# Sixteen experts on tiles of 64 slots instead of 128, two tiles side by side on TensorE's columns, in six streams that keep an expert's weights

## The chip, the cores and the metric

The kernel runs on one core of one Trainium2 chip. The metric is the device time of one execution in microseconds (us). A core has five engines that work at the same time and meet at semaphores: PE (TensorE, matrix products), DVE (VectorE), ACT (ScalarE), POOL (GpSimd) and SP, which mostly starts DMAs. PEld in the profile is the loading of PE's stationary operand. All numbers are float32 unless a row says otherwise. A float32 matmul shows up in the trace as two records, each with its own weight load; a transpose on PE shows up as one.

## The reference, cut to what matters

The program is one block of a graph network on 1250 nodes of 512 numbers: a performer block and a four-layer graph network, whose results are added to `x`, and then a mixture of experts. Only the last part is touched by the change:

```python
h = xf @ shared_w1 + shared_b1                      # shared expert, 384 hidden units
z = swiglu5(h, *shared_act) @ shared_w2 + shared_b2
gate_probs = softmax(xf @ gate_w + gate_b)          # 16 experts
w, idx = top_k(gate_probs, 2); w = w / sum(w)
he = einsum('nd,edh->enh', xf, expert_w1) + expert_b1     # w1: 512 x 768 per expert
te = swiglu5(he, expert_act)                        # gate and up are the even and odd columns
oe = einsum('enh,ehd->end', te, expert_w2) + expert_b2    # w2: 384 x 512 per expert
y = einsum('ne,end->nd', cw, oe)                    # cw: the two weights of a node, else 0
return y + z
```

Two experts per node are wanted, so 2500 rows (node, expert) have to be computed. With the inputs of the reference the gate is far from even. Rows by expert, 0 to 15: 71, 5, 1044, 7, 450, 335, 0, 2, 12, 2, 1, 13, 245, 0, 313, 0. That makes 29 tiles of 128 rows or 49 tiles of 64 rows, each tile of one expert.

## The kernel before, in words

The order of the work on each engine is written out by hand: each engine has its own list of instructions, and semaphores join them. Nothing is reordered by a scheduler.

`moe` has four parts. (1) Routing: `gate_pe`, `choose_dve`, `rank_pe` and `slots_dve` find each node's two experts, count the rows of each expert, round each count up to tiles, and give each row a slot. `slot_expert` holds, for each of the `SLOT_TILES` tiles, the number of its expert. POOL scatters the 2500 rows into `slot_dram` with 20 indirect DMAs (L1998). (2) Meanwhile PE computes the shared expert (`shared_pe`, L2179, and `shared_down_pe`, L2231 and L2233). (3) The expert loop, one tile per round. (4) The combination: the two results of each node are read back and added with their weights (L2438).

There are always 35 rounds in part 3, the most that any routing could need, and tiles beyond the last real one are computed too, with the last expert's weights. In round `i` of `experts_pe`, PE does: the first 512 columns of the up product of tile `i+1` (`up_pe`, L2306), the three transposes of tile `i`'s gated values (L2326), the other 256 up columns of tile `i+1` (L2306), the four transposes that turn the rows of tile `i+2` into columns (L2293), and the down product of tile `i` (L2337). `glu_dve` (L2350 to L2359) adds the bias, clips, and multiplies; `experts_act` makes the sigmoid (L2375) and the three copies out of PSUM (L2366, L2388, L2394); POOL scatters the tile's result (L2407). SP loads for every tile the expert's `w1` and `w2`, its bias row copied to 128 partitions, and its five constants (`load_up`), into rings of `U = 3` buffers, and the tile's rows (`load_slots`) into a ring of 10. It loads the weights again even where two tiles in a row are of the same expert.

The performer, a quite different part of the program, has one product (`attend`, L942) that puts two 64-column outputs on PSUM partitions 0 to 63 and 64 to 127, with different stationary and different moving operands, in turn.

Of the kernel before, what the change touches and what calls it, by code (L numbers as in the profile page):

```python
# [18 lines left out]
N = 1250  # L19
# [33 lines left out]
SLOT_TILES = (2 * N + EXPERTS * 127) // 128  # L53
# [58 lines left out]
def build(nc, a, out):  # L112
    with ExitStack() as ctx:
# [5 lines left out]
        slot_dram = nc.dram_tensor("slot_rows", [SLOT_TILES * 128, ROW], F32)  # L119
        outer = lambda name, shape: ctx.enter_context(nc.sbuf_tensor(name, shape, F32))  # L120
        w = [outer(f"w{i}", [128, KC, D]) for i in range(3)]
# [11 lines left out]
        with c.stage():  # L133
            moe(c, x, w, cols, rows, slot_dram, out)


def performer(c, xbuf, gnn_x, xn_dram, sum_dram, ln_count, cond_parts, cond_w_parts, w, cols, rows,
# [66 lines left out]
    with ExitStack() as ctx:  # L204
# [45 lines left out]
        blank = kf[0:112].rearrange("p a f -> p (a f)")[:, 0:ROW]  # L250
# [83 lines left out]
        def sp_start():  # L334
# [24 lines left out]
            for r0 in (0, 64):  # L359
# [4 lines left out]
            load(sp, slot_dram[:, :].rearrange("(p s) d -> p s d", p=112),  # L364
                 blank.unsqueeze(1).broadcast_to([112, SLOT_TILES * 128 // 112, ROW])).then_inc(c.slots_blank, 16)
# [949 lines left out]
def gnn(c, x, ln_count, cond_parts, cond_w_parts, w, y_cols, rows, sum_dram):  # L1315
# [28 lines left out]
    with ExitStack() as ctx:  # L1344
# [87 lines left out]
        def norm_dve(m, t):  # L1432
# [11 lines left out]
            if t >= 1:  # L1444
# [4 lines left out]
                if m == 2 * L - 1:  # L1449
                    v.wait_ge(norm_step, done + 1)  # L1450
                    v.tensor_scalar(v_rows[:, s, :], x[:, s, :], mv[:, s, 0:1], rstd[:, s:s + 1], ALU.subtract,
                                    ALU.mult).then_inc(normed, 1)
                    return
# [19 lines left out]
        def layer_sp(l):  # L1473
# [20 lines left out]
            if last:  # L1494
# [3 lines left out]
                for n, done in enumerate(((o_mm, NT * L), (h_mm, 12 * L))):  # L1498
                    sp.wait_ge(*done)
                    load(sp, w[n][:].rearrange("p c o -> p (c o)")[:, 0:4 * FFN_I].rearrange("p (c o) -> p c o", c=2),  # L1500
                         a["L0_ffn_shared_w1"].rearrange("(c p) o -> p c o", p=128)[:, 2 * n:2 * n + 2, :]).then_inc(
# [352 lines left out]
def moe(c, x, w, cols, rows, slot_dram, out):  # L1854
# [4 lines left out]
    U, S, R = SLOT_RING, SLOT_TILES, NT  # L1859
    TE = NT * EXPERTS  # L1860
    RANK, TOTAL, LOGIT, TURN, OUT = 6, 7, 5, 6, 7
    param_dram = nc.dram_tensor("swiglu_params", [EXPERTS + 1, 8], F32)
    back_dram = nc.dram_tensor("slot_outputs", [2 * N + S * 128, D], F32)
# [13 lines left out]
    up_in = [c.sem(f"e_up_in{u}") for u in range(U)]  # L1877
    down_in = [c.sem(f"e_down_in{u}") for u in range(U)]
# [7 lines left out]
    with ExitStack() as ctx:  # L1886
        sb = lambda name, shape, dt=F32: ctx.enter_context(nc.sbuf_tensor(name, shape, dt))
        ring = lambda name, shape: [sb(f"{name}{i}", shape) for i in range(U)]
        hidden = sb("m_hidden", [128, IC, N])
        ew1 = ring("m_ew1_", [128, KC, 2 * FFN_I])  # L1890
        ew2 = ring("m_ew2_", [128, IC, D])
# [20 lines left out]
        slot_id = sb("m_slot_id", [1, S])  # L1912
# [3 lines left out]
        ones = sb("m_ones", [P, P])  # L1916
        start_of = sb("m_start_of", [P, NT + 1, EXPERTS])
        place = sb("m_place", [P, NT, EXPERTS])
        total = sb("m_total", [P, EXPERTS])
        tiles_of = sb("m_tiles_of", [P, 3, EXPERTS])  # L1920
        pos_f = sb("m_pos_f", [P, 2, NT])
        pos = sb("m_pos", [P, 2 * NT], U32)
        passed = sb("m_passed", [1, S, EXPERTS])
        expert_f = sb("m_expert_f", [1, S])
        slot_expert = sb("m_slot_expert", [1, S], I32)
        slot_place = sb("m_slot_place", [128, S], I32)
        place_of = sb("m_place_of", [P, 2, NT])
        blank_place = sb("m_blank_place", [128, S])
# [577 lines left out]
```

## Time and profile before

| | us |
|---|---|
| Median of 3 runs (2779.07 to 2780.36) | 2779.67 |
| The profiled execution's own time | 2776.7 |
| Its span | 2775.0 |
| PE busy in it | 2667.2 |
| DVE busy | 1432.7 |
| ACT busy | 858.1 |
| POOL busy | 294.7 |

Busy times are sums over the span of one execution; PE's is that of pipelined matmuls whose ends are modelled, so a PE busy all the time is not shown to be at its peak. The rows further down are read with the line numbers of the kernel before. "us" after a start time is how long the merged instructions took, "xN" how many there are, and square brackets hold the engine's idle time ahead of the row and what ended it.

### The profile page before, as it was taken

How to read it: one execution, taken by the hardware profiler on the slowest of the kernel's cores; microseconds unless marked ns; L12 is line 12 of the kernel's file. 1: busy time of each engine (PE TensorE's matmuls, PEld its weight loads, DVE VectorE, ACT ScalarE, POOL GpSimd, SP SyncE). 2: the span in 40 equal slices, each digit the busy share in tenths (PEclk: the TensorE clock that was granted, in tenths of full speed). 3: DMA queues.
4: the chain of work that ended last, by engine and by line, in shares of the span. 5: the costliest groups of instructions: out<-in, count | busy, mean ns of one | idle time of the engine just before them, and what ended most of it. 6: DMA issues, size and time to landing. Idle time of an engine off the chain costs nothing. (4 is left out here: it accounts for less than half of the span.)

```text
span 2775.0 us, 28828 instructions
## 1 busy us (share of the span) xinstructions
PE 2667.2 (96%) x10335; PEld 1613.8 (58%) x10336; DVE 1432.7 (52%) x3252; ACT 858.1 (31%) x1813; POOL 294.7 (11%) x308
## 2 busy tenths in 40 slices
PE   7999889989999999999999999999999999999995
PEld 4554544435777555677655577655577754455552
DVE  8995651322666551566652466553366544433333
ACT  5654533210444211244211144312044322212221
POOL 3000012000200100100020200020010013311111
PEclk9999999999999999999999999999999999999997
DMA  5400101230000010000011100011000011669996
GB/s 165 147 21 11 38 8 45 69 106 31 23 1 1 21 37 31 23 1 1 0 39 35 37 2 1 1 39 34 32 7 1 1 46 31 235 232 391 389 378 226
DMA packets 105293, 203.78 MB, mean 73 GB/s; under 512 B 22273, under 2 KB 22803, under 8 KB 105151
## 3 DMA queue, kind: packets, MB, share of 16 engines
q1 hardware_dynamic: 94858, 182.11, 18.8%
q0 software_dynamic: 7600, 14.93, 1.5%
q10 hardware_dynamic: 2693, 4.89, 0.6%
q8 instruction: 84, 1.38, 0.2%
q14 instruction: 58, 0.48, 0.1%
HBM read 168.18 MB, written 31.66 MB: 72 GB/s over the span
## 5 line engine op out<-in xcount | busy, mean ns | idle before, releaser
L1784 ACT ACTIVATE g_prob<-g_prob,g_row_max 125x1250 f32<-125x1250 f32 x160 | 214.0, 1337 | 710.6 <-DVE g_row_max L1718 710.6
L1524 PE MATMUL psum<-cols,w 128*128 128x500 f32 (+1 forms) x1152 | 408.2, 514 | 6.8 <-PEq L81 6.8
L1586 PE MATMUL psum<-g_k_cols,g_q_cols 128*125 128x512 f32 (+1 forms) x960 | 362.9, 513 | 1.9 <-DVE g_row_max L1715 1.9
L1600 PE MATMUL psum<-cols,rows 125*128 125x250 f32 x1600 | 364.0, 374 | 0.1
L1524 PEld LDWEIGHTS psum<-cols,w 128*128 128x128 f32 x1152 | 216.5, 189 | 186.6 <-issue 178.5
L1600 PEld LDWEIGHTS psum<-cols,rows 125*128 125x128 f32 x1600 | 302.6, 189 | 34.7 <-issue 3.8
L1715 DVE CUSTOM_DVE_ANT_0 g_prob<-psum,ln_count 125x1250 f32<-125x1250 f32 x160 | 233.4, 1459 | 75.0 <-PE psum L1586 75.0
L1586 PEld LDWEIGHTS psum<-g_k_cols,g_q_cols 128*125 128x125 f32 x960 | 168.0, 187 | 161.8 <-issue 159.1
L1725 DVE COPY cols<-psum 125x500 f32<-125x500 f32 x160 | 108.6, 678 | 198.8 <-PE psum L1615 198.8
L1615 PEld LDWEIGHTS psum<-ident,g_prob 125*125 125x125 f32 x1600 | 199.4, 188 | 9.0 <-issue 1.9
L1615 PE MATMUL psum<-ident,g_prob 125*125 125x125 f32 x1600 | 200.3, 272 | 0.0
L2306 PE MATMUL psum<-m_ew,m_x_cols 128*128 128x256 f32 (+1 forms) x560 | 191.9, 486 | 0.3 <-ACT m_x_cols L2366 0.3
L1838 POOL TENSOR_TENSOR xbuf<-xbuf,g_bias_rows 125x512 f32<-125x512 f32 x40 | 67.4, 1721 | 937.4 <-DVE rows L1460 937.4
L1690 DVE TENSOR_SCALAR g_k_cols<-psum,g_bias_cols 128x500 f32<-128x500 f32 (+1 forms) x48 | 31.3, 653 | 237.4 <-PE psum L1524 237.4
L1708 DVE TENSOR_SCALAR g_prob<-g_prob,g_row_max 125x1250 f32<-125x1250 f32 x160 | 145.5, 909 | 5.6
L2306 PEld LDWEIGHTS psum<-m_ew,m_x_cols 128*128 128x128 f32 x560 | 103.7, 190 | 72.5 <-issue 66.5
L1626 PE MATMUL psum<-w,g_q_cols 128*125 128x512 f32 x320 | 143.9, 592 | 0.0
L1672 PE MATMUL psum<-w,g_k_cols 128*125 128x512 f32 x320 | 143.6, 592 | 0.0
L1800 ACT COPY cols<-psum 125x500 f32<-125x500 f32 x320 | 134.3, 469 | 17.6 <-PE psum L1615 16.9
L1573 PE MATMUL psum<-w,cols 128*125 128x512 f32 x320 | 139.3, 592 | 0.0
L2350 DVE TENSOR_TENSOR m_work<-psum,m_eb 128x768 f32<-128x768 f32 x35 | 33.5, 958 | 173.4 <-PE psum L2306 173.4
L1834 POOL TENSOR_TENSOR xbuf<-xbuf,g_bias_rows 125x512 f32<-125x512 f32 x40 | 55.2, 1417 | 616.2 <-DMA g_bias_rows<-in_L_gnn_bo 616.2
(317 smaller groups left out, 3282.9 us busy)
## 6 DMA issues: line engine op xcount, KB each, us to landing
m_ew<-in_L_ffn_expert_w SPq DMA_DIRECT2D x35, 1536.0 KB
m_ew<-in_L_ffn_expert_w SPq DMA_DIRECT2D x35, 768.0 KB, 7.9
m_eb<-in_L_ffn_expert_b SPq DMA_DIRECT2D x35, 384.0 KB
slot_rows<-p_kf SPq DMA_DIRECT2D x1, 9240.0 KB, 34.1
rows<-slot_rows SPq DMA_DIRECT2D x35, 264.0 KB, 8.1
w<-in_L_gnn_m_w SPq DMA_DIRECT2D x8, 1024.0 KB
w<-in_L_mix_W SPq DMA_DIRECT2D x4, 1024.0 KB, 5.1
w<-in_L_gnn_wq SPq DMA_DIRECT2D x4, 1024.0 KB, 5.2
```

What stands on the lines that cost most here:

```text
L1524: ins = c.pe.matmul(c.bank(group_bank(g), width), wt[:, k, o * 128:(o + 1) * 128], y_cols[:, k, start:start + width], start=(k == 0), stop ...
L1573: ins = pe.matmul(c.bank(V_BANKS[t], D, P), y_cols[:, k, t * P:(t + 1) * P], w[2][:, k, :], start=(k == 0), stop=(k == KC - 1))
L1586: ins = pe.matmul(psum[0:P, start:start + width], q_cols[:, h, t * P:(t + 1) * P], k_cols[:, h, start:start + width], start=True, stop=True)
L1600: ins = pe.matmul(c.bank(6 + g % 2, 2 * P), v_rows[:, j, h * 128:(h + 1) * 128], turned_prob[:, g % 2, j, :], start=(j == 0), stop=(j == N ...
L1615: ins = pe.transpose(psum[0:P, b * BANK + j * P:b * BANK + (j + 1) * P], prob[:, u, (j0 + j) * P:(j0 + j + 1) * P], ident[0:P, 0:P])
L1626: ins = pe.matmul(c.bank(t % 2, D, P), q_cols[:, k, t * P:(t + 1) * P], w[0][:, k, :], start=(k == 0), stop=(k == KC - 1))
L1672: ins = pe.matmul(c.bank(t % 2, D, P), k_cols[:, k, t * P:(t + 1) * P], w[2][:, k, :], start=(k == 0), stop=(k == KC - 1))
L1708: v.tensor_scalar(prob[:, u, :], prob[:, u, :], row_max[:, u, 3:4], None, ALU.mult).then_inc(prob_made, 1)
L1715: v.tensor_tensor_reduce(prob[:, u, :], psum[0:P, 0:N], ln_count[:, t, :], 1.0, NOT_AN_EDGE / 10, ALU.add, ALU.max, row_max[:, u, 0:1]).th ...
L1784: s.activation(prob[:, u, :], prob[:, u, :], ACT.Exp, bias=row_max[:, u, 1:2], accum_out=row_max[:, u, 2:3]).then_inc(exp_made, 1)
L1800: s.copy(turned_prob[:, g % 2, j0:j0 + nj, half:half + P], by_chunk(c.bank(b, nj * P, P))).then_inc(turned_act, 1)
L2306: ins = pe.matmul(psum[0:128, at:at + cn], x_cols[u][:, k, :], ew1[u][:, k, c0:c0 + cn], start=(k == 0), stop=(k == KC - 1))
```

## The change

Tiles have 64 slots (`HALF`) in place of 128. There are `STREAMS = 6` streams of `TURNS = 9` tiles, 54 tiles in all, of which 49 are real. The tiles lie in order of expert, and stream `s` has tiles `9s` to `9s+8`. A round of the expert loop now treats a pair: the same turn of two neighbouring streams, on columns 0 to 63 and 64 to 127 of PE. There are 27 pairs; pair `i` is of streams 0 and 1, 2 and 3, or 4 and 5 by `i` modulo 3.

By the counts above the streams hold these experts:

```
stream 0: 0 0 1 2 2 2 2 2 2        stream 3: 4 4 5 5 5 5 5 5 7
stream 1: 2 2 2 2 2 2 2 2 2        stream 4: 8 9 10 11 12 12 12 12 14
stream 2: 2 2 3 4 4 4 4 4 4        stream 5: 14 14 14 14 15 15 15 15 15
```

Each stream has one buffer for `w1` and `w2` of its expert. The first six are loaded by SP (`load_first_weights`); the buffers of streams 3 to 5 lie in memory that the shared expert uses before, so SP loads stream 3 after the shared up product and streams 4 and 5 after the shared down product. From then on POOL issues for every tile but a stream's last one indirect gather for `w1` after the pair's up product and one for `w2` after its down product. Where the next tile has the same expert, 127 of the 128 row numbers are made too large and are skipped, so that one row of 12 KB or 6 KB is still moved. For this the rows of `w1` and `w2` go to partitions in runs ("(p c)" in place of "(c p)"), and the layer norm ahead permutes its output columns to match. The biases are now loaded in two halves of 64 partitions, the rows in two halves too. The bias add writes gate and up values apart, so the clips after it read runs.

```diff
+HALF = 64
+STREAMS = 6
+TURNS = -(-((2 * N + EXPERTS * (HALF - 1)) // HALF) // STREAMS)
+SLOT_TILES = STREAMS * TURNS
...
-            for i in range(SLOT_TILES):
+            for i in range(PAIRS):
...
             for k in range(KC):
-                ins = pe.matmul(psum[0:128, at:at + cn], x_cols[u][:, k, :], ew1[u][:, k, c0:c0 + cn], start=(k == 0),
-                                stop=(k == KC - 1))
+                for e, s in enumerate(streams(i)):
+                    ins = pe.matmul(psum[lanes(e), at:at + cn], x_cols[u][:, k, lanes(e)], ew1[s][:, k, c0:c0 + cn],
+                                    start=(k == 0), stop=(k == KC - 1))
...
                 for k in range(IC):
-                    ins = pe.matmul(c.bank(OUT), t_cols[u][:, k, :], ew2[u][:, k, :], start=(k == 0),
-                                    stop=(k == IC - 1))
+                    for e, s in enumerate(streams(i)):
+                        ins = pe.matmul(psum[lanes(e), OUT * BANK:OUT * BANK + D], t_cols[u][:, k, lanes(e)],
+                                        ew2[s][:, k, :], start=(k == 0), stop=(k == IC - 1))
...
-            v.tensor_tensor(h[u][:], psum[0:128, at:at + 2 * FFN_I], eb1[u][:], ALU.add).then_inc(e_biased, 1)
+            v.tensor_tensor(by_half(h[u]), by_unit(psum[0:128, at:at + 2 * FFN_I]), by_unit(eb1[u][:]), ALU.add).then_inc(
+                e_biased, 1)
...
+            def next_weights(i, into, from_, ready):
+                for s in streams(i):
+                    j = tile_of(s, turn(i) + 1)
+                    g.indirect_dma_start(
+                        out=into[s].rearrange("p c o -> p (c o)"), out_offset=None, in_=from_,
+                        in_offset=bass.IndirectOffsetOnAxis(ap=weights_of[:, j:j + 1], axis=0),
+                        bounds_check=EXPERTS * 128 - 1, oob_is_err=False).then_inc(ready[s], 16)
...
+                if turn(i) + 1 < TURNS:
+                    g.wait_ge(up_mm, i + 1)
+                    next_weights(i, ew1, w1_rows, next_w1_in)
+                    g.wait_ge(down_mm, i + 1)
+                    next_weights(i, ew2, w2_rows, next_w2_in)
                 g.wait_ge(place_made, 2 * i + 2)
                 g.wait_ge(out_made, i + 1)
...
+            for s in range(3):
+                load_first_weights(s)
             for i in range(U):
-                load_up(i)
+                load_bias(i)
             sp.wait_ge(scattered, 16 * 2 * NT)
             for i in range(R):
                 load_slots(i)
+            sp.wait_ge(h_mm, 2 * len(GROUPS))
+            load_first_weights(3)
+            sp.wait_ge(s_mm, NT)
+            load_first_weights(4)
+            load_first_weights(5)
```

`slots_dve` also computes, on 128 partitions, the row numbers for the gathers (`weights_of`): six small DVE instructions more, and the two that compare tiles with experts treat 864 numbers in place of 560. The fill of `slot_dram` with blank rows, early in the program, is of 3456 rows in place of 4480.

PE in the expert loop, before, one round (`m_ew` are the experts' weights, `m_x_cols` the rows turned to columns, `m_t_cols` the gated values turned, `m_work` those before):

```order
L2306 MATMUL psum<-m_ew_0,m_x_cols 128x512 x4
L2326 MATMUL psum<-ident,m_work 128x128 x3
L2306 MATMUL psum<-m_ew_0,m_x_cols 128x256 x4
L2293 MATMUL psum<-ident,rows 128x128 x4
L2337 MATMUL psum<-m_ew_2,m_t_cols 128x512 x3
```

The same of the changed kernel, a round whose up product has streams 4 and 5 (one of the weight buffers lies in `w`, another in `cols`):

```order
L2397 MATMUL psum<-ident,m_work 128x128 x3
L2377 MATMUL psum<-m_ew,m_x_cols 64x256 x8
L2362 MATMUL psum<-ident,rows 128x128 x4
L2410 MATMUL psum<-w,m_t_cols 64x512
L2410 MATMUL psum<-m_ew,m_t_cols 64x512
L2410 MATMUL psum<-w,m_t_cols 64x512
L2410 MATMUL psum<-m_ew,m_t_cols 64x512
L2410 MATMUL psum<-w,m_t_cols 64x512
L2410 MATMUL psum<-m_ew,m_t_cols 64x512
L2377 MATMUL psum<-m_ew,m_x_cols 64x512
L2377 MATMUL psum<-cols,m_x_cols 64x512
```

Each full-width matmul has become two of 64 output columns, in turn for the two streams; the transposes stay whole, and the down product is followed at once by the next up product, both in halves.

POOL in the expert loop, before (three instructions for a tile):

```order
L2401 TENSOR_TENSOR m_blank_place<-rows,m_blank_place 128x1
L2404 CAST m_slot_place<-m_blank_place 128x1
L2407 DMA slot_outputs<-m_work,m_slot_place 6980x512
```

And of the changed kernel, for one pair:

```order
L2485 TENSOR_TENSOR m_blank_place<-rows,m_blank_place 128x1
L2488 CAST m_slot_place<-m_blank_place 128x1
L2477 DMA w<-in_L_ffn_expert_w,m_weights_of 128x3072
L2477 DMA m_ew<-in_L_ffn_expert_w,m_weights_of 128x3072
L2477 DMA w<-in_L_ffn_expert_w,m_weights_of 128x1536
L2477 DMA m_ew<-in_L_ffn_expert_w,m_weights_of 128x1536
L2496 DMA slot_outputs<-m_work,m_slot_place 5956x512
```

The four gathers have come in ahead of the scatter of the pair's result; SP's queue has lost the weight loads in exchange and has twice the small ones.

## Rows read from the trace of the kernel before

**Rows 1.** The page: PE's busy time, and DMA busy tenths in 40 slices.
```profile
PE 2667.2 (96%) x10335; PEld 1613.8 (58%) x10336; DVE 1432.7 (52%) x3252; ACT 858.1 (31%) x1813; POOL 294.7 (11%) x308
...
DMA  5400101230000010000011100011000011669996
```

**Rows 2.** Windows: stretch, length, busy us by engine, PE clock, DMA share, GB/s.
```profile
2550.00:2600.00 50.00, 50.00 (x173) 28.67 (x172) 17.53 (x28) 13.34 (x24) 8.36 (x18) 1.00 1.02 389
```

**Rows 3.** Timeline of PE, one round of the expert loop: start, us, instructions.
```profile
2567.80 3.60 PE L2306 MATMUL psum<-m_ew,m_x_cols 128*128 128x512 f32 x8
2571.24 0.49 PE L2326 MATMUL psum<-ident,m_work 128*128 128x128 f32 x3
2571.56 1.89 PE L2306 MATMUL psum<-m_ew,m_x_cols 128*128 128x256 f32 x8
2573.29 0.60 PE L2293 MATMUL psum<-ident,rows 128*128 128x128 f32 x4
2573.73 2.74 PE L2337 MATMUL psum<-m_ew,m_t_cols 128*128 128x512 f32 x6
2576.31 3.60 PE L2306 MATMUL psum<-m_ew,m_x_cols 128*128 128x512 f32 x8
```

**Rows 4.** Timeline of PE, the first and the last product of the loop.
```profile
2443.08 8.86 PE L2306 MATMUL psum<-m_ew,m_x_cols 128*128 128x512 f32 x24 [0.29 <-ACT m_x_cols L2366]
...
2739.76 2.84 PE L2337 MATMUL psum<-m_ew,m_t_cols 128*128 128x512 f32 x6 [0.57 <-ACT m_t_cols L2388]
```

**Rows 5.** Timeline of PE in the performer: two outputs of 64 columns in turn.
```profile
340.26 1.91 PE L942 MATMUL psum<-p_shared 128*64 128x250 f32 x16
342.10 1.13 PE L874 MATMUL psum<-p_pmat,p_q_cols 64*125 64x256 f32 x8
```

**Rows 6.** Timeline of PE, shared expert: 16 records of full width.
```profile
2390.09 3.55 PE L2179 MATMUL psum<-cols,w 128*128 128x250 f32 x16
2393.47 0.38 PE L2157 MATMUL psum<-ident,m_cw 125*16 125x125 f32 x2
```

**Rows 7.** Timelines of DVE and PE: from up product to the transposes.
```profile
2726.57 0.96 DVE L2350 TENSOR_TENSOR m_work<-psum,m_eb 128x768 f32<-128x768 f32 x1 [4.98 <-PE psum L2306]
...
2729.47 0.62 DVE L2359 SCALAR_TENSOR_TENSOR m_work<-m_work,m_eprm 128x384 f32<-128x384 f32 x1
...
2732.81 0.49 PE L2326 MATMUL psum<-ident,m_work 128*128 128x128 f32 x3
```

**Rows 8.** DMA issues, 2500 to 2700 us: count, KB each, us to landing.
```profile
m_ew<-in_L_ffn_expert_w SPq DMA_DIRECT2D x24, 1536.0 KB
m_ew<-in_L_ffn_expert_w SPq DMA_DIRECT2D x24, 768.0 KB, 7.9
m_eb<-in_L_ffn_expert_b SPq DMA_DIRECT2D x24, 384.0 KB
rows<-slot_rows SPq DMA_DIRECT2D x20, 264.0 KB, 8.4
slot_outputs<-m_work,m_slot_place POOLq DMA_INDIRECT x24, 6.9
```

**Rows 9.** DMA queues, 2500 to 2700 us: packets, MB, share of 16 engines.
```profile
q1 hardware_dynamic: 31819, 70.88, 93.9%
q0 software_dynamic: 1840, 6.03, 7.4%
```

**Rows 10.** POOL's indirect DMAs: timeline, groups of 2400:2775, and one line.
```profile
2371.50 1.67 POOL L1998 DMA_INDIRECT slot_rows<-rows,m_pos  x1 [0.30 <-issue]
2373.47 1.18 POOL L1998 DMA_INDIRECT slot_rows<-rows,m_pos  x1 [0.30 <-issue]
...
L2407 POOL DMA_INDIRECT slot_outputs<-m_work,m_slot_place x35 | 35.1, 1004 | 276.0 <-ACT m_work L2394 276.0
...
L443 POOL DMA_INDIRECT p_q_cols<-in_src,tile_rows x5: 952/963/1280, 14.7 to 20.1; - x5
```

**Rows 11.** Timeline of SP: the first tiles' rows.
```profile
2414.49 4.92 SPq L95 DMA_DIRECT2D rows<-slot_rows  x10
```

More of the change, by code:

```diff
@@ L133, in build @@
         with c.stage():
-            moe(c, x, w, cols, rows, slot_dram, out)
+            moe(c, x, w_all, cols, rows, slot_dram, out)
 def performer(c, xbuf, gnn_x, xn_dram, sum_dram, ln_count, cond_parts, cond_w_parts, w, cols, rows,
@@ L1850, in gnn, with moe @@
             layer_pool(l)
-def moe(c, x, w, cols, rows, slot_dram, out):
+def moe(c, x, w_all, cols, rows, slot_dram, out):
     nc, psum, ident, a = c.nc, c.psum, c.ident, c.a
     U, S, R = SLOT_RING, SLOT_TILES, NT
+    PAIRS = S // 2
+    SIDES = STREAMS // 2
+    SKIP = 4096.0
+    W1_COLS, W2_COLS = KC * 2 * FFN_I, IC * D
     TE = NT * EXPERTS
@@ L1933, in moe @@
         t_cols = [t_all[:, u] for u in range(U)]
+        x_flat = x_all[:].rearrange("p u c n -> p (u c n)")
+        passed = x_flat[:, 0:S * EXPERTS].rearrange("p (s e) -> p s e", e=EXPERTS)
+        expert_f, same, weights_f = (x_flat[:, S * (EXPERTS + n):S * (EXPERTS + n + 1)] for n in range(3))
         turned_logit = x_all[0:EXPERTS].rearrange("p u c n -> p (u c n)")[:, 0:N]
@@ L1937, in moe @@
         scratch = [work[:, i * 1500:(i + 1) * 1500].rearrange("p (n c) -> p n c", n=3) for i in range(2)]
-        w_flat = [v[:].rearrange("p c o -> p (c o)") for v in w]
+        w_flat = [w_all[:, n].rearrange("p c o -> p (c o)") for n in range(3)]
+        weights = [ew[0][:], ew[1][:], ew[2][:], cols[:].rearrange("p c n -> p (c n)"),
+                   w_all[:].rearrange("p n c o -> p (n c o)"), ew[3][:]]
+        ew1 = [v[:, 0:W1_COLS].rearrange("p (c o) -> p c o", c=KC) for v in weights]
+        ew2 = [v[:, W1_COLS:W1_COLS + W2_COLS].rearrange("p (c o) -> p c o", c=IC) for v in weights]
+        w1_rows = a["L0_ffn_expert_w1"].rearrange("e (p c) o -> (e p) (c o)", c=KC)
+        w2_rows = a["L0_ffn_expert_w2"].rearrange("e (p c) o -> (e p) (c o)", c=IC)
+        by_unit = lambda v: v.rearrange("p (q k n) -> p q k n", k=IC, n=2)
+        by_half = lambda v: v.rearrange("p (n k q) -> p q k n", n=2, k=IC)
+        side = lambda i: i % SIDES
+        turn = lambda i: i // SIDES
+        streams = lambda i: (2 * side(i), 2 * side(i) + 1)
+        tile_of = lambda s, q: s * TURNS + q
+        lanes = lambda e: slice(e * HALF, (e + 1) * HALF)
         w1 = [w_flat[n][:, 0:4 * FFN_I].rearrange("p (c o) -> p c o", c=2) for n in range(2)]
-        w2 = w[2][:, 0:IC, :]
+        w2 = w_all[:, 2, 0:IC, :]
         cols_flat = cols[0:P].rearrange("p c n -> p (c n)")
@@ L2267, in load_slots @@
                 sp.wait_ge(place_made, 2 * (i - R) + 1)
-            load(sp, rows[:, i % R, :], slot_dram[i * 128:(i + 1) * 128, :]).then_inc(slot_in[i % R], 16)
+            for e, s in enumerate(streams(i)):
+                j = tile_of(s, turn(i))
+                load(sp, rows[lanes(e), i % R, :], slot_dram[j * HALF:(j + 1) * HALF, :]).then_inc(slot_in[i % R], 16)
         def experts_sp():
@@ L2300, in up_pe @@
                 pe.wait_ge(x_made, i + 1)
-                pe.wait_ge(up_in[u], 48 * rounds(i))
+                for s in streams(i):
+                    pe.wait_ge(*((next_w1_in[s], 16 * turn(i)) if turn(i) else (first_w1_in[s], 16)))
                 if i >= 2:
@@ L2316, in experts_pe @@
             up_pe(0, BANK, 2 * FFN_I - BANK)
-            for i in range(SLOT_TILES):
+            for i in range(PAIRS):
                 u = i % U
-                if i + 1 < SLOT_TILES:
+                if i + 1 < PAIRS:
                     up_pe(i + 1, 0, BANK)
@@ L2345, in glu_dve @@
             v.wait_ge(up_mm, i + 1)
[L2346 removed]
+            v.wait_ge(bias_in[u], 64 * rounds(i))
             if i >= U:
@@ L2382, in experts_act @@
             sigmoid(0)
-            for i in range(SLOT_TILES):
+            for i in range(PAIRS):
                 u = i % U
@@ L2461, in dve_program @@
             shared_down_dve()
-            for i in range(SLOT_TILES):
+            for i in range(PAIRS):
                 glu_dve(i)
```

161 lines of the change are left out of this document (96 added, 65 removed).

## The prediction

> **What bounds the kernel now.** I read the page first. PE is busy 96% of the span, and the DMA engines, nearly idle for most of it, are full in the last slices [rows 1]. Those are the expert loop. The windows there show PE busy all 50 us at the full granted clock and DMA at 1.02 of its 16 engines at once, with 389 GB/s [rows 2]. Two resources are full, so which one sets the pace? PE's timeline answers it. A round runs from 2567.80 to 2576.31, 8.50 us, with no idle time between its pieces: 3.43 us for the 512 up columns, 0.32 for three transposes, 1.73 for the other 256, 0.44 for four transposes, 2.58 for the down product (start to start) [rows 3]. PE waits for no weights. The DMA engines are full because 1536 + 768 + 384 + 264 KB come in and 256 KB (128 rows of 2 KB) go out per round [rows 8], 3.29 MB in 8.50 us, 387 GB/s: just what they carry. The loop lasts from 2443.08 to 2739.76 + 2.84 = 2742.60 [rows 4], 299.5 us, which is 34 rounds of 8.50 and 10.5 us of start and end.
>
> DVE and ACT are not near it. DVE starts the bias add of a tile at 2726.57 and ends the last multiply at 2730.09, and PE wants the result at 2732.81 [rows 7]: 2.7 us to spare per round.
>
> **The change on PE.** What was one matmul is now two of half width over the same number of streamed columns. If they ran one behind the other, the products would take twice as long. The performer has this very form: 64 output columns, 128 rows, float32, in turn on both halves of PSUM's partitions, each with its own moving operand. Its 16 records over 250 columns take 342.10 - 340.26 = 1.84 us [rows 5], where 16 records of full width over 250 columns take 2393.47 - 2390.09 = 3.38 us [rows 6]. So the halves do run side by side. Against half of 3.38, 1.69 us, a section pays 0.15 us more. I read this as the stagger of the first and last record, which have no partner, and let it grow with the streamed width: 0.15 us for the section of 256 columns and 0.30 for that of 512. Down product and next up product follow each other in halves and are one section. A pair then takes 8.50 + 0.15 + 0.30 = 8.95 us. The bounds are 8.50 (no stagger shows) and 9.25 (down and up products pay each for itself).
>
> The TensorE page of the Trainium skill, "TensorE: Matmul & The Clock Gate", Part 3, has three column tiles of 32 speed up 2.38 times, 0.79 of three. If two tiles did as badly, 1.59 times, the products of a pair, 15.5 us one behind the other, would take 9.7 us and the pair 10.5. The rows here show 3.38 / 1.84 = 1.84 times, so I keep 8.95 and give the other a small chance below.
>
> 27 pairs replace 35 tiles: 26 x 8.95 + 10.5 + 0.45 for the last section = 243.7 us in place of 299.5, **55.8 us less**. Only the number of rounds and the stagger count here. PE's weight loads, half as wide and twice as many, lie beside matmuls as they do in the performer.
>
> **The weights.** 12 times a stream's expert changes, and six are loaded first: 18 x 2304 KB in place of 35. The total falls from 3212 KB a tile to 908 KB a pair and 42 MB of weights, far below what 27 x 8.95 us can carry. But the changes come together. Between turn 1 and turn 2 four streams change (0, 2, 3, 4), so in that turn's 26.9 us (three pairs) DMA must move 4 x 2304 + 3 x 908 KB = 12.2 MB, 31.4 us at 389 GB/s. The next turn has three changes, 9.9 MB and 25.4 us, and fits. I add **4 us** for weights that come late, between 0 and 8.
>
> Does the gather's queue carry as much? In the loop before, the software queue moved 6.03 MB with 7.4% of the engines over 200 us, 407 GB/s of a full share, and the hardware queue 70.88 MB with 93.9%, 377 GB/s [rows 9]. It does, at 2 KB rows.
>
> **POOL.** It gets four gathers per pair ahead of the scatter. A scatter of 125 rows takes 1.18 us and 0.30 to the next, that of 128 rows of 2 KB 1.00, a gather of 90 rows of 500 bytes 0.96 [rows 10]. All three are near 1 us though bytes differ sixfold, so I take 1.18 + 0.30 for a gather of 128 rows of 12 KB or 6 KB too: 5.9 us, with the scatter 1.3 and two small operations 0.5 (estimated from their 0.2 us each) 7.7 us of 8.95. POOL keeps up, barely. In order it waits for the down product of pair i, issues two gathers, scatters, and only then issues the `w1` gathers of pair i+1, some 8 us after that pair's up product (3.3 until the down product of pair i ends, 4.7 of POOL's own work). PE wants them three pairs less 5.9 us after the same point, at 21: 13 us for at most 3.1 MB, 8.1 us at 389 GB/s. The scatter's landing is wanted three rounds later and had 6.9 us [rows 8]. Below, the price of a dearer gather: POOL sets the pace once a gather takes over 1.5 us.
>
> The page "SBUF — State Buffer" of the Trainium skill (its note on the trap where DVE blocks DMA) says that POOL cannot write descriptors while DVE runs a two-port operation, which speaks against moving loads from SP to POOL, and the clips now read runs and could enter that mode. The trace has one scatter at 1.67 us while DVE was busy, against 1.18 [rows 10]. With 0.49 us on each of five indirect DMAs a pair would take POOL 10.1 us and the time would be 28 us above my forecast. DVE has two such operations of under 0.5 us in a round, so I expect a tenth of that.
>
> **What costs nothing, and under what cover.** The bias add writes with a large step; even at twice its 0.96 us the chain fits the 2.7 us. DVE's longer `slots_dve` adds some 2 us ahead of the shared expert's work, and the scatter shifts by under 1 us; the first tiles' rows were asked for at 2414.49 [rows 11] and are wanted at 2441. SP now issues 20 loads there in place of 10 (4.9 us more) before stream 3's weights, about 2424 to 2432, wanted at 2449. Streams 4 and 5 start at 2441; stream 5's `w1` ends 3.9 MB later, 10 us plus some 2, at 2454; PE wants it after two up products and a down product, about 2458. Cover: 4 us. The tail after 2742.60 is the same.
>
> **Sum.** -55.8 + 4 = -51.8 us on the profiled execution's 2776.7: 2724.9. The median of the runs lies 3.0 us above that execution, so **2728 us**.
>
> **Rivals.**
> - Weights late in earnest (chance 0.14). A turn's weights come behind each other and behind POOL's own order. For it: the change asks for 12.2 MB in 26.9 us. Against: all other turns need less. If rows of 12 KB ran at half of 389 GB/s, the three turns with 4, 3 and 2 changes would take about 55, 43 and 31 us for 26.9 each: 48 us late, 2772. Half of that, 2750, is the likelier.
> - POOL becomes the bound (0.10), the one that ends slower. Place: the gathers in `experts_pool`. If its time follows bytes as between the gather of 44 KB (0.96) and the scatter of 264 KB (1.18) [rows 10], 0.001 us per KB, the `w1` gather takes 2.45 us and `w2` 1.68, a pair 11.3 us, the loop 24 x 11.3 + 3 x 8.95 + 7 = 305 us and 4 for late weights: 2789. If it were fully proportional (7.0 and 3.5 us), about 3090. It decides from a mean of 2.3 us a gather, where a pair takes 11.1 us and the gain is gone. Against: the scatter of 256 KB took 1.00, less than that of 264 KB.
> - The halves don't overlap (0.04): 8.50 + 3.43 + 1.73 + 2.58 = 16.24 us a pair, 440 us, 2921. Against it stand only [rows 5], but in the same form.
> - They overlap as the rule has it (0.05): 10.5 us a pair, 26 x 10.5 + 12 = 285, 14 less than before: 2765.
>
> **The numbers.** My forecast has 0.67, with its own range of 2711 (8.50 a pair, nothing late) to 2743 (9.25, 8 us late). 8 in 10 takes in most of the first and last rival: 2709 to 2768. A time within 0.2% (5.6 us) of 2779.67 would count as no change. Faster 0.85 (forecast, the rule's overlap, nearly all of late weights), slower 0.12 (POOL, no overlap), same 0.03.
>
> **What would show it.** PE's timeline: L2377 sections of 16 records at 512 columns near 3.7 us; 7.4 would be no overlap. Pair period 8.95 us away from turns 1 to 4, longer with idle time before L2377 "<-DMA" at the pairs of streams 2 and 3 in turn 2. POOL: L2477 at about 1.2 us; over 1.5, the period is POOL's. DMA share in the loop near 0.7, from 1.02. The forecast is wrong if every pair, also those with no change of expert, has PE idle.

## The result, and the profile after

The changed kernel takes 2743.91 us (median of 4 runs, 2741.16 to 2744.92) against 2780.02 us before: ratio 0.9869, 95% interval 0.9852 to 0.9886. It is faster, by 36.1 us where 52 were forecast. The time lies in the wide range (2709 to 2768) and 1 us above the forecast's own (2711 to 2743). The profiled execution took 2741.16 us with a span of 2739.3.

The page after, PE's busy time, DMA in 40 slices and the two large queues:

```profile
PE 2618.9 (96%) x10697; PEld 1545.9 (56%) x10698; DVE 1429.3 (52%) x3218; ACT 838.6 (31%) x1781; POOL 383.4 (14%) x382
...
DMA  5300101130000001100011000001000001469736
...
q1 hardware_dynamic: 60282, 106.18, 12.1%
q0 software_dynamic: 20784, 41.85, 4.7%
```

Against [rows 1] the DMA engines are full (a digit of 9) in one slice and no longer in three. Windows after (us of the stretch, busy us of each engine, granted clock, DMA share, GB/s): the loop, then 50 us near its end, 27 us in its first third, and 4 us right behind a wait:

```profile
2442.90:2707.00 264.10, 251.05 (x1369) 101.58 (x1369) 98.72 (x135) 59.50 (x106) 135.10 (x174) 0.98 0.64 208
2650.00:2700.00 50.00, 50.00 (x286) 20.64 (x284) 19.27 (x26) 11.82 (x21) 25.59 (x35) 1.00 0.49 161
2485.00:2512.00 27.00, 23.80 (x122) 9.04 (x118) 8.66 (x13) 5.51 (x10) 16.82 (x21) 0.94 1.02 341
2507.00:2511.00 4.00, 4.00 (x12) 1.41 (x13) 0.00 (x0) 0.00 (x0) 2.76 (x5) 0.57 1.03 325
```

The loop takes 264.1 us in place of 299.5 [rows 4]. It starts 0.2 us earlier than before, and the 32.3 us behind it are the same in both, so this one stretch holds the result. It has two kinds of pair. Near the end PE is busy all the time at the full clock, as in [rows 2]. Here is PE's timeline of one such pair, cut to the first records of each piece, which answers to [rows 3] and [rows 5]:

```profile
2638.39 0.59 PE L2377 MATMUL psum<-w,m_x_cols 128*64 128x512 f32 x1
2638.40 0.59 PE L2377 MATMUL psum<-m_ew,m_x_cols 128*64 128x512 f32 x1
2638.82 0.59 PE L2377 MATMUL psum<-w,m_x_cols 128*64 128x512 f32 x1
...
2641.93 0.55 PE L2397 MATMUL psum<-ident,m_work 128*128 128x128 f32 x3
2642.41 0.43 PE L2377 MATMUL psum<-w,m_x_cols 128*64 128x256 f32 x1
...
2644.28 0.66 PE L2362 MATMUL psum<-ident,rows 128*128 128x128 f32 x4
2644.87 0.64 PE L2410 MATMUL psum<-m_ew,m_t_cols 128*64 128x512 f32 x1
...
2647.50 2.74 PE L2377 MATMUL psum<-m_ew,m_x_cols 128*64 128x512 f32 x12
```

The two halves start 0.01 us apart and the next two 0.43 us later: they run side by side, without a stagger. The pair takes 9.11 us (9.10 in most). Against [rows 3], the pieces are 3.54 us (3.43), 0.48 (0.32), 1.87 (1.73), 0.59 (0.44) and 2.63 (2.58). Each piece that ends at a change of width, from full to half or back, has grown by 0.11 to 0.16 us, 0.60 us in all with the small rest on the down product.

The other kind of pair lies between 2497 and 2593 us. PE's timeline at the first wait:

```profile
2506.88 0.61 PE L2377 MATMUL psum<-m_ew,m_x_cols 128*64 128x512 f32 x1 [3.20 <-DMA cols<-in_L_ffn_expert_w,m_weights_of]
2506.89 0.66 PE L2377 MATMUL psum<-cols,m_x_cols 128*64 128x512 f32 x1
2507.33 1.01 PE L2377 MATMUL psum<-m_ew,m_x_cols 128*64 128x512 f32 x1
...
2508.13 1.06 PE L2377 MATMUL psum<-m_ew,m_x_cols 128*64 128x512 f32 x1
...
2508.98 1.06 PE L2377 MATMUL psum<-m_ew,m_x_cols 128*64 128x512 f32 x1
```

PE was idle for 3.20 us, since a gather of `w1` had not landed, and then its records stand 0.85 us apart in place of 0.43. The granted clock is 0.57 over these 4 us, most of them at the lower level (1.2 GHz). The list of waits over the loop (us in total, times, longest) has the gathers at its head; beside them stand 3.2 us of short waits at the loop's two ends:

```profile
PE psum L2377 <- DMA m_ew<-in_L_ffn_expert_w,m_weights_of: 6.8, 3, 3.0
...
PE psum L2377 <- DMA cols<-in_L_ffn_expert_w,m_weights_of: 3.2, 1, 3.2
```

From the starts of the up products, the pairs of this stretch took 16.6 us more than 9.10 each. 10.0 of these are the four waits (3.20, 2.96, 1.67, 2.14). Behind the first, the second and the last of them PE's work at the lower clock took 1.75 us more each, 5.3 in all. The other 1.3 are delays of 0.05 to 0.30 us around the waits, too short for the list. By place: 10.0 us of lateness in turn 2, 2.5 in turn 3 and 4.1 in turn 4.

The DMA queues while the late gathers ran (2485 to 2512 us) answer to [rows 9]:

```profile
q0 software_dynamic: 1312, 7.70, 83.0%
q1 hardware_dynamic: 1044, 1.47, 19.0%
```

With all 16 engines full they carried 341 GB/s in sum, not 389 [rows 2]. Last, groups in the loop on POOL (the first also holds `w1` and `w2` rows mixed), which answer to [rows 10], and the page's line of the bias add on DVE:

```profile
L2477 POOL DMA_INDIRECT m_ew<-in_L_ffn_expert_w,m_weights_of x64 | 65.7, 1027 | 101.6 <-PE psum L2410 54.0 <-PE psum L2377 29.5 <-issue 18.1
L2496 POOL DMA_INDIRECT slot_outputs<-m_work,m_slot_place x26 | 26.7, 1028 | 19.8 <-ACT m_work L2468 12.5 <-issue 7.3
```

```profile
L2423 DVE TENSOR_TENSOR m_work<-psum,m_eb 128x768 f32<-128x768 f32 x27 | 41.0, 1517 | 151.6 <-PE psum L2377 144.7
```

A gather costs POOL 1.03 us, and the bias add went from 0.96 to 1.52 us, under cover but in the first and the last pair.

### The profile page after: what moved, and what is told of

Read it like the earlier page. It is cut to its first block and busy times, and to the rows that moved or that the text cites. A ratio compares the mean times of both kernels' runs of the same rounds, so it can differ in the third digit from the quotient of the medians.

```text
span 2739.3 us, 29622 instructions
## 1 busy us (share of the span) xinstructions
PE 2618.9 (96%) x10697; PEld 1545.9 (56%) x10698; DVE 1429.3 (52%) x3218; ACT 838.6 (31%) x1781; POOL 383.4 (14%) x382
## 5 line engine op out<-in xcount | busy, mean ns | idle before, releaser
L2377 PE MATMUL psum<-m_ew,m_x_cols 128*64 128x256 f32 (+1 forms) x576 | 154.6, 499 | 3.7 <-DMA cols<-in_L_ffn_expert_w,m_weights_of 3.2
L2423 DVE TENSOR_TENSOR m_work<-psum,m_eb 128x768 f32<-128x768 f32 x27 | 41.0, 1517 | 151.6 <-PE psum L2377 144.7
L784 DVE TENSOR_SCALAR p_shared<-iota,edge_cols 125x250 f16<-125x250 f16 x400 | 114.5, 287 | 0.0
```

Of the source, the lines that this page charges most:

```text
L2377: ins = pe.matmul(psum[lanes(e), at:at + cn], x_cols[u][:, k, lanes(e)], ew1[s][:, k, c0:c0 + cn], start=(k == 0), stop=(k == KC - 1))
```

## The experiments

Loop lengths below are from the first up product's start to the last down product's end, in the profiled execution. "Late" is what the pairs take beyond the undisturbed one, summed (the first full pair, 0.84 us longer in the changed kernel whatever its weights do, is left out). Two executions of like kernels can differ by 1.6 us at either end of the loop: where the granted clock fell at its start (0.63 to 0.70 over 4 us) the first 33 records took 7.4 us and not 5.8, and where it fell in the last pair (0.57) the last product was as much longer. Each kernel ran beside the kernel before, whose medians were 2779.61 us for the first four, 2780.05 for the next four, 2777.09 for the last three; so ratios are compared across these groups, not times.

| kernel | pair | late | loop | median us | ratio (interval) |
|---|---|---|---|---|---|
| before | 8.50 | 0 | 299.5 | 2780.0 | 1 |
| changed | 9.10 | 16.6 | 264.1 | 2743.91 | 0.9869 (0.9852 to 0.9886) |
| weights never change | 9.10 | 0 | 249.2 | 2730.08 | 0.9816 (0.9799 to 0.9833) |
| streams one after the other | 11.78 | 0 | 318.3 | 2800.68 | 1.0070 (1.0053 to 1.0086) |
| `w1` a pair earlier | 9.10 | 11.7 | 259.3 | 2736.15 | 0.9841 (0.9825 to 0.9858) |
| two changes of width | 8.80 | 24.3 | 266.1 | 2741.94 | 0.9862 (0.9846 to 0.9879) |
| all gathers in full | 14 to 17 | | 401 | 2885.83 | 1.0392 (1.0368 to 1.0417) |
| stream 4 from its far end | 9.10 | 6.6 | 255.8 | 2736.27 | 0.9844 (0.9824 to 0.9865) |
| before, weights left out | 8.50 | 0 | 301.2 | 2779.29 | 1.0001 (0.9991 to 1.0010) |
| the three edits | 8.80 | 6.5 | 246.6 | 2727.33 | 0.9821 (0.9801 to 0.9841) |
| `w1` earlier, scatter first | 9.10 | 9.5 | 260.4 | 2737.04 | 0.9852 (0.9837 to 0.9867) |
| three edits, scatter first | 8.80 | 0.2 | 240.3 | 2723.13 | 0.9807 (0.9794 to 0.9820) |
| far end, two changes | 8.80 | 12.2 | 252.2 | 2730.32 | 0.9826 (0.9813 to 0.9840) |

**The weights never change.**

```diff
-            v.tensor_tensor(same[:, 1:], expert_f[:, 1:], expert_f[:, 0:S - 1], ALU.is_equal)
+            v.tensor_tensor(same[:, 1:], expert_f[:, 1:], expert_f[:, 1:], ALU.is_equal)
```

> The changed kernel, but every tile after a stream's first counts as of the same expert, so each gather moves one row and an expert's weights never change (the output is then that of the first six experts' weights only). PE's instructions and POOL's are the same in number. Theory (the loop is 27 pairs of 9.10 us plus weights that come late, 16.6 us of them in seven pairs): all pairs take 9.10 us, no wait of PE for a gather, 16 to 17 us less than the changed kernel, 2727 us. Rival 1 (the longer pairs come from POOL or from the bias add, not from the bytes of weights): the time stays at 2744. Rival 2 (part of the 9.10 us is itself contention with the weight traffic): pairs go to 8.95 or less and the time to below 2723.

All pairs behind the first took 9.10 us and no wait on a gather was left: the loop was 249.2 us, 14.9 less, and it would be 16.5 less but for its last product, which ran at the lower clock here. The late weights are the cause of the disturbed pairs, the slow records included. Even so each pair stays at 9.10, not 8.95, so the other 0.15 us per pair has nothing to do with the weights' traffic.

**The streams one after the other**, all of one half's matmuls before the other's, in both products.

```diff
-            for k in range(KC):
-                for e, s in enumerate(streams(i)):
+            for e, s in enumerate(streams(i)):
+                for k in range(KC):
...
```

> The changed kernel with the two loops exchanged: the matmuls of one stream over all rows of the product, then those of the other, in place of taking turns. Same instructions, same bytes. Theory (the halves overlap only where they are issued in turn, since PE takes its matmuls in order): nearly all overlap goes, a pair takes 9.10 + 7.7 = 16 to 17 us, late weights vanish, the loop takes about 440 us and the kernel 2905 to 2930. Rival (two matmuls on different halves overlap however they are ordered, or PE looks ahead): within 20 us of 2744.

The pair took 11.78 us, which neither expectation had. PE's timeline, one section of 256 columns:

```profile
2602.59 1.29 PE L2377 MATMUL psum<-m_ew,m_x_cols 128*64 128x256 f32 x5
2603.51 0.43 PE L2377 MATMUL psum<-cols,m_x_cols 128*64 128x256 f32 x1
2603.72 0.38 PE L2377 MATMUL psum<-m_ew,m_x_cols 128*64 128x256 f32 x1
2603.77 0.38 PE L2377 MATMUL psum<-cols,m_x_cols 128*64 128x256 f32 x1
```

The second stream's first record starts after four of the first's eight, 0.92 us in, and from there the two run side by side. So records of different halves overlap even where they don't alternate in the program, but only the last few of one with the first of the other. The expectation had PE take its matmuls in order. Their starts do not keep to it here: three records of the first stream start (from 2603.72) after the second stream's first (2603.51), which stands behind them in the program. Taking turns is worth 2.68 us a pair; without it the change would be slower than before.

**The first matrices' gathers a pair earlier.**

```diff
...
+                if i + 1 < PAIRS and turn(i + 1) + 1 < TURNS:
+                    g.wait_ge(up_mm, i + 2)
+                    next_weights(i + 1, ew1, w1_rows, next_w1_in)
                 if turn(i) + 1 < TURNS:
-                    g.wait_ge(up_mm, i + 1)
-                    next_weights(i, ew1, w1_rows, next_w1_in)
```

> The changed kernel with POOL's gathers in another order: the w1 gathers of pair i+1 are issued as soon as its up product is done, ahead of the w2 gathers and the scatter of pair i, some 8 us earlier than now. Same bytes. Theory A (PE waits because the w1 gathers are issued late, 13 us before they are wanted): the 16.6 us of late weights fall below 5, 2730 to 2733 us. Theory B (PE waits because the bytes of turns 1 to 4 are more than the DMA engines carry, at 340 GB/s): the waits of turn 2, 8.5 us of the 16.6, stay, and only those of turn 4 go, 2737 to 2741 us. No effect at all would speak against both.

No wait on a gather was left on PE, yet 11.7 us stayed late, by a wait that neither theory named. The waits of DVE:

```profile
DVE m_work L2423 <- DMA slot_outputs<-m_work,m_slot_place: 37.8, 5, 10.4
```

The wait has moved. DVE may not overwrite its buffer until the scatter of three pairs before has landed, and this stands behind gathers of megabytes in POOL's one software queue; PE then waits for DVE (3.97, 2.06 and 2.22 us). The DMA engines were full here too, 319 GB/s from 2485 to 2540, so this run does not show whether the order in the queue or the full engines made the scatter late. The lateness of turn 4 is gone.

**Two changes of width in a pair**: the transposes of the rows come ahead of the narrower up section, so the two sets of transposes stand together.

```diff
                 ins.then_inc(turned, 1)
-                if i + 1 < PAIRS:
-                    up_pe(i + 1, BANK, 2 * FFN_I - BANK)
                 if i + 2 < PAIRS:
                     turn_slots_pe(i + 2)
+                if i + 1 < PAIRS:
+                    up_pe(i + 1, BANK, 2 * FFN_I - BANK)
```

> The changed kernel with the four transposes of the rows moved ahead of the last 256 up columns, so that all seven transposes stand together: two changes between full and half width per pair in place of four. Same instructions. In the trace the four changes of a pair cost 0.11 to 0.16 us each over the round of before, 0.60 in all. Theory A (each change of width costs 0.15 us, whatever streams): a pair goes from 9.10 to 8.80 us, 8 us less over 27 pairs, 2736 us, if weights come no later for it. Theory B (the cost is a stagger that grows with the streamed columns, as forecast): only the section of 256 columns goes, 0.15 us a pair, 4 us less. Rival: the transposed values reach PE later or its copies wait, and the gain is lost.

PE's timeline of an undisturbed pair from the transposes on:

```profile
2643.34 0.55 PE L2397 MATMUL psum<-ident,m_work 128*128 128x128 f32 x3
2643.72 0.60 PE L2362 MATMUL psum<-ident,rows 128*128 128x128 f32 x4
2644.25 0.43 PE L2377 MATMUL psum<-w,m_x_cols 128*64 128x256 f32 x1
...
2646.03 0.59 PE L2410 MATMUL psum<-m_ew,m_t_cols 128*64 128x512 f32 x1
```

The pair takes 8.80 us, 0.30 less for two changes less: half of the 0.60 us. By the Trainium skill, "TensorEngine Tiling (Array Packing)", Key Properties, a change of tiling mode drains TensorE; it gives no price. The trace agrees in that each change costs 0.15 us; that a drain is what costs it, no run shows. Yet the time did not fall by 8 us: its ratio, 0.9862, is within the interval of the changed kernel's 0.9869. The waits on gathers rose from 10.0 to 17.4 us and all lateness from 16.6 to 24.3, 7.7 more for 7.8 saved (26 pairs of 0.30): a shorter pair leaves less time for the same bytes. While weights are late, DMA sets the pace and what PE saves there is lost.

**All gathers in full**: the comparison that finds an expert unchanged is made false.

```diff
-            v.tensor_tensor(same[:, 1:], expert_f[:, 1:], expert_f[:, 0:S - 1], ALU.is_equal)
+            v.tensor_tensor(same[:, 1:], expert_f[:, 1:], expert_f[:, 1:], ALU.not_equal)
```

> Every gather after a stream's first fetches both matrices in full, whether the expert changed or not: 48 full gathers of each matrix instead of the few of the streams' changes. Theory (the weights come late because the gathers are bound by the rate at which they are carried, which was 341 GB/s while they ran in the changed kernel): a pair then carries 2 x 2304 KB of weights and some 0.9 MB of rows and results, 5.65 MB, which is 16.6 us at 341 GB/s, against 9.10 us of TensorE. For 24 pairs that is 24 x 7.5 = 180 us over a loop without late weights: 2728 + 180 = 2908 us (2880 to 2950), with the DMA engines full all through the loop. First rival (the gathers could run at the 389 GB/s of the loads of the kernel before): 14.5 us per pair, 2857 us. Second rival (what costs is TensorE's clock, at half after each idle stretch, and not the transfers alone): every pair is then computed at the half clock, some 17 us of TensorE, and the waits come on top of a part of it, 2950 us or more, with a granted clock near 0.6 in the loop.

A window of its loop, and POOL's group of gathers:

```profile
2550.00:2600.00 50.00, 35.70 (x159) 13.26 (x155) 12.44 (x18) 8.00 (x14) 16.41 (x22) 0.83 1.02 357
```

```profile
L2477 POOL DMA_INDIRECT m_ew<-in_L_ffn_expert_w,m_weights_of x64 | 64.6, 1010 | 186.6 <-PE psum L2410 137.8 <-PE psum L2377 30.7 <-issue 18.1
```

DMA sets the pace, at 357 GB/s, between the 341 of the theory and the 389 of the old loads: 2885.83 us between the two forecasts. The granted clock was 0.83 and not near 0.6, so the second rival did not come true. At this rate 5.65 MB take 15.8 us. Keeping the weights is thus what makes tiles of 64 slots pay: without it the kernel is 4% slower than before. And a full gather costs POOL 1.01 us, no more than one that skips 127 rows of 128 (1.01 in the kernel whose weights never change).

**Stream 4 from its far end**, so that the turns hold 1, 3, 2, 1, 1, 1, 1 and 2 changes, not up to four.

```diff
-        tile_of = lambda s, q: s * TURNS + q
+        tile_of = lambda s, q: s * TURNS + (TURNS - 1 - q if s == 4 else q)
...
```

> Stream 4 takes its tiles from its far end, so that its expert changes at other turns: the turns hold 1, 3, 2, 1, 1, 1, 1 and 2 changes in place of four in the second. Theory (lateness is what a turn's bytes take beyond its 27.3 us, at 341 GB/s): the fullest turn carries 9.8 MB, 28.7 us, 1.4 us late, the others fit, so of the 16.6 us that the loop loses 3 to 5 stay: 2732 us (2729 to 2736), and only one or two waits on a gather in the loop. Rival (a gather is late by itself, since it is issued only after the product that frees its buffer and has some 6 to 7 us until the next pair but two needs it, however few there are in a turn): each turn keeps its wait, 2741 to 2746 us, as the changed kernel.

One wait was left, of 3.64 us, and 2.75 us of slow records behind it: 6.6 us late of 16.6. A gather is not late by itself, as the rival had it: where few change together there is no wait. The wait of turn 4 is gone too; in the changed kernel both streams of one pair change there, here only one of them does. The wait that is left is at the pair of streams 2 and 3 in turn 2, where again both change. The size was off again: three changes in a turn are not the 1.4 us that its bytes give.

**The kernel before with its weights left out.**

```diff
+            part = slice(0, 128 if i < U else 1)
-            load(sp, ew1[u][:], a["L0_ffn_expert_w1"][ds(e, 1), :, :].rearrange("l (c p) o -> p (l c) o", p=128))
+            load(sp, ew1[u][part], a["L0_ffn_expert_w1"][ds(e, 1), :, :].rearrange("l (c p) o -> p (l c) o", p=128)[part])
...
```

> The kernel before, with the weights of tiles 3 to 34 cut to one partition's rows: the changes of weights are left out, so nearly all of the loop's bytes are gone. Theory (the old loop is bound by TensorE, whose rounds of 8.50 us follow each other without a gap, and its DMA engines, full as they are, cost it nothing): the loop of 35 rounds stays within 2 us of 299.5 us, and the time within 2776 to 2782 us. So keeping the weights is worth nothing by itself, and all of the change's gain comes of the fewer rounds. Rival (the full DMA engines slow TensorE's reads or delay rows and biases now and then): over 5 us faster, 2774 us or less.

Its window answers to [rows 2]:

```profile
2550.00:2600.00 50.00, 50.00 (x172) 28.56 (x171) 17.42 (x30) 13.27 (x23) 8.39 (x18) 1.00 0.37 112
```

DMA fell from 389 to 112 GB/s and the time did not move. The loop of 301.2 us is 1.7 longer than before since it started at the lower clock here. The full DMA engines cost the old loop nothing, so all of the gain comes of 27 rounds in place of 35.

**The three edits together.**

> Three edits of the changed kernel together: stream 4's tiles from its far end, the first matrices' gathers issued one pair earlier, and the hidden layer's transposes put ahead of the narrower up product so that TensorE changes between full and half width twice in a pair. Theory (the costs are separate: 9.10 to 8.80 us per pair, and late weights that go with the burst): 2744 - 27 x 0.30 - 13 = 2723 us, down to 2719 if nothing is late (2718 to 2730), undisturbed pairs of 8.80 us. Rival (whatever is taken off TensorE comes back as lateness, since a shorter pair leaves less time for the same bytes, and the results' scatter stays behind the gathers in its queue): 2733 us or more, with waits of VectorE on the scatter of three pairs before.

2727.33 us. Four waits of DVE on the scatter stayed, and with them 6.5 us. The costs are separate, as the theory has it; what the rival foresaw is only what is left.

**The scatter ahead of the second matrices' gathers**, first with the earlier gathers alone, then with all three edits.

```diff
-                    next_weights(i, ew2, w2_rows, next_w2_in)
                 g.wait_ge(place_made, 2 * i + 2)
                 g.wait_ge(out_made, i + 1)
                 g.indirect_dma_start(
...
+                if turn(i) + 1 < TURNS:
+                    next_weights(i, ew2, w2_rows, next_w2_in)
```

> The kernel with the first matrices' gathers one pair earlier (2736 us), with one more edit: GpSimd issues a pair's scatter of results ahead of the gathers of the second matrices and no longer behind them. Theory (the stalls that were left there, some 11.6 us, are VectorE's wait for a scatter that stands in its queue behind up to 2.4 MB of second matrices, 7 us at 341 GB/s): the scatter lands up to 7 us sooner, the waits of 10.4 us at most shrink to 4 or less, which the two pairs between take up, and of the 11.6 us at most 4 stay: 2728 us (2724 to 2732). Rival (the scatter is late because the first matrices' gathers of the next pair, issued before it, are also in its way, or because the 16 DMA engines are full whatever the order is): the waits on the scatter stay, or become waits on the second matrices, 2734 us or more.

> All three edits (stream 4 from its far end, first matrices one pair earlier, two changes of width in a pair), and the scatter ahead of the second matrices' gathers. Theory (of the 2727.3 us of the three edits, 6.5 us were left as waits on the scatter): 26 pairs of 8.80 us without a stall, 2727.3 - 6.5 = 2721 us (2717 to 2724). Rival (the bytes of the fullest turn, which are issued in any order, are late all the same): a stall of 4 us or more stays in the third turn, 2725 us or more.

With four changes in one turn it brought nothing (ratio 0.9852 against 0.9841, intervals that overlap). The waits of DVE and PE there:

```profile
DVE m_work L2423 <- DMA slot_outputs<-m_work,m_slot_place: 37.7, 5, 10.6
PE psum L2377 <- DMA m_ew<-in_L_ffn_expert_w,m_weights_of: 6.1, 2, 4.2
```

The scatter is as late as before, and a `w1` gather is late as well: where the bytes of a turn don't fit, their order only chooses who waits. With the changes spread the same edit removed the last stall:

```profile
2441.60:2682.00 240.40, 237.23 (x1369) 102.16 (x1369) 97.73 (x135) 55.90 (x107) 137.85 (x174) 1.00 0.73 228
```

Its loop is all pairs of 8.80 us with 0.2 us late, 240.3 us. The median of 2723.13 us is 54.0 us below that of before beside it, and the ratio, 0.9807, is the lowest of all, though its interval overlaps that of the three edits alone: this version beats both kernels. It is 2 us over what the theory gave.

**Far end and two changes of width, without the earlier gathers.**

> Stream 4 from its far end and two changes of width in a pair, without the earlier gathers. Theory (the two are separate, as long as a turn's bytes fit: 8.80 us instead of 9.10 in all pairs but those of the fullest turn, which waits 6.5 us or a little more): 2736.3 - 27 x 0.30 = 2728 us (2725 to 2732). Rival (a width change saved comes back as lateness, as it did with the four changes in one turn, where 8 us saved came out as 2): 2733 us or more, with more or longer waits on gathers than the 3.64 us of the kernel with stream 4 alone.

2730.32 us, near the theory's 2728, but it is half the rival's: lateness rose from 6.6 to 12.2 us, with two waits (2.8 and 4.4 us) in place of one. The spread alone doesn't give slack enough for the faster pair; with the earlier gathers 6.5 us stay late, and 0.2 once the scatter goes first too.

## Why the prediction was right, and where 16 us went

In the profiled executions the loop was to be 51.8 us shorter and was 35.4 shorter. The missing 16.4 us are two terms of the sum.

- **Rounds and overlap: right.** 27 pairs for 35 tiles, halves side by side. The rival with a pair of 10.5 us fell: a pair of 512-column matmuls takes 0.43 us, as one of full width did.
- **"I read this as the stagger": wrong, 3.9 us.** The forecast had 0.15 us in a section of 256 columns and 0.30 in that of 512, 8.95 us a pair. There is no stagger. The cost is at each change of width, on entering the halves as on leaving them, whatever the width streamed: four times 0.15. [Rows 5] held only the exit. The entry was in the performer's line ahead of it, in the kernel before:

```profile
339.28 1.05 PE L927 MATMUL psum<-ident,p_kf 125*128 125x125 f32 x8
```

  Eight transposes take 0.98 us to the next start at 340.26, where eight at the pace of the three in [rows 3] (0.32 us) would take 0.85. 26 pairs x 0.15 = 3.9 us; the kernel with two changes confirms the price.
- **"I add 4 us for weights that come late": 16.6, so 12.6 us off.** The cause was right: skipping all gathers takes away all of it. The place was right in part: 10.0 us fell in turn 2, the one with four changes, but 2.5 fell in turn 3 and 4.1 in turn 4, which the sum had as fitting. Three steps of the sum failed. The rate was read from loads in another queue (389 GB/s); with the gathers it was 341, and 12.2 MB then take 35.8 us, 8.5 more than three pairs, of which the waits of turn 2 show 6.5. The claim that the gather's queue carries as much rested on rows of 2 KB; why it carried less here was not tried. Each longer wait left PE at half its clock for a while, 5.3 us that the sum did not have. And "13 us for at most 3.1 MB" left out what runs beside the `w1` gathers. The wait of turn 4 shows it; its two `w1` gathers were issued at 2567.72 and 2569.07:

```profile
2552.00:2567.00 15.00, 14.63 (x84) 6.32 (x86) 3.63 (x5) 2.75 (x5) 8.35 (x12) 1.00 0.32 93
2567.72:2582.04 14.32, 12.18 (x68) 4.62 (x65) 7.13 (x10) 4.06 (x7) 8.52 (x11) 1.00 0.96 334
```

  The DMA engines were a third busy until just before, and then 4.78 MB moved in 14.3 us until PE could go on at 2582.04: the `w2` gathers, the scatter, rows and biases came with the 3.1 MB. This wait comes of the bytes of one pair and of the time of their issue, and not of the bytes of a turn; in the kernel with `w1` a pair earlier it is gone.
- **Lateness in earnest as a rival (2750)**: it was named, and the time lies between it and the forecast, nearer to the rival (6 us) than to the forecast (16). Its premise, rows of 12 KB at half rate, was wrong.
- **The upper end of the range**: 26 x 9.25 + 10.5 + 0.75 + 8 us for the loop gives 2740 us and not 2743. So the case that the forecast held to be its worst is passed by 4 us: the pair stayed within its bounds (9.10 of 9.25), the lateness did not (16.6 of 8).
- **POOL: right.** Gather 1.03 + 0.30 us against 1.18 + 0.30 forecast, whatever its bytes: the dearer gather, the only case of slower with a large share, fell. POOL is busy 135 of 264 us. (The rival's limit was worked out wrong: a pair of 11.1 us comes of 2.0 us a gather, not 2.3.) By the Trainium skill, "SBUF — State Buffer", the note on the trap where DVE blocks DMA, DVE's two-port operations keep POOL from writing descriptors. It cost next to nothing here: the 53 gathers that ran beside a DVE instruction of any kind took 1.04 us on the mean, the other 43 1.00.
- **Cover of the small edits: right.** The bias add's 1.52 us (forecast: at most 1.92) shows only in the first and the last pair, where the transposes wait 0.77 and 1.57 us (0.18 and 1.04 before). Streams 4 and 5 had their first weights in time: the pair at 2458.00 starts without a wait.
- **"DMA share near 0.7"**: 0.64. "3.7 us a section" of 512 columns: 3.54.

That three of the four waits bring the lower clock is seen in the rows; that it would not come without the idle time is shown by the kernel whose weights never change. Its price, 1.75 us a time, is read from the pairs behind the waits; it was not tried by itself.

## What to carry to other kernels

Two tiles of 64 columns side by side give the full factor of two if the halves take turns in the program, and each change between half and full width costs about 0.15 us: put the full-width work together. An average of bytes over a loop says little; sum them over the span in which a buffer must be filled, at the rate of the queue that carries them, and expect an idle TensorE to lose a second time by its clock. Do the same sum for a single pair, from the issue of its gathers to their use, with all that runs beside them. Where the bytes of a stretch don't fit, moving a gather earlier only moves the wait; spread the bytes first, then order the queue.

## What the hardware showed that I had not expected

- Matmuls on different halves of the columns overlap without taking turns, by up to four records at either side (11.78 us a pair, where one behind the other 16.2 were expected); their starts then don't follow the program's order.
- An indirect gather costs POOL 1.0 us with 128 rows of 12 KB, 128 rows of 6 KB, or one row and 127 skipped.
- With all 16 DMA engines full, loads of SP carried 389 GB/s, gathers with the rest 319 to 357.
- A scatter of 256 KB lay behind gathers long enough for DVE to wait 10.4 us for it. By the Trainium skill, "DMA: Bandwidth & Descriptors", SWDGE vs HWDGE vs iDMA, GpSimd's transfers share one software queue; the waits here agree, though full engines alone would delay it too.
- Short idle times brought PE's granted clock down to the lower of its two levels, and their length alone does not say when. It fell around all waits of 2.14 to 7.26 us inside the loop, the kernel with all gathers in full aside, and around none of those of 1.07 to 2.06 us. But in the kernel with all gathers in full it stayed up behind one of 2.47 us, and after the 1.57 us in the last pair it fell in three kernels (weights never change; two changes of width; `w1` earlier, scatter first) and not in the changed one.
